# A two-layer attention and expert kernel: the first attention's first loads moved ahead of a phase seam, its router softmax split in two, and semaphore releases gathered

## What is computed

```python
x = L0_attn_x                                     # (2, 2048, 256)
xn = layernorm(x)
s = attention_full(xn, w_qkv, b_qkv, w_o) + xn    # 16 heads of 16, scale 1/sqrt(256)
g = silu(experts_bilinear(xn, router, ...))       # two branches, 8 experts of rank 64, cumulative sums
x = x + s * g
xn = layernorm(x)
s = attention_band(xn, w_qkv, b_qkv, w_out)       # keys within 64 positions, scale 1/4
g = silu(lora_experts(xn, gate_w, lora_U, lora_V))
return x + s * g
```

## Time and profile before

| | us |
|---|---|
| median of 3 runs | 2449.58 |
| lowest and highest of them | 2440.53, 2459.89 |
| the profiled execution, its own time | 2435.89 |
| its span in the trace | 2433.9 |
| first projection, about | 44 to 212 |
| full attention with its prologue | 213 to 1653 |
| prologue until the last of the first 32 maxima | 213 to 267 |
| combine of the experts | 1653 to 1970 |
| second projection, band attention, last combine | 1970 to 2070, to 2332, to 2434 |

### The profile page before, as it was taken

How to read it: one execution, slowest core, us unless ns; L and a number is a source line. 1 busy time by engine, 2 the same in 40 slices (tenths; PEclk the granted TensorE clock), 3 DMA queues, 4 the chain that set the end, 5 groups by cost and what they waited for, 6 DMA issues and landing times. The chain is left out here.

```text
span 2433.9 us, 43647 instructions
## 1 busy us (share of the span) xinstructions
PE 2211.6 (91%) x14912; PEld 1233.1 (51%) x14912; DVE 1838.5 (76%) x3240; ACT 1442.2 (59%) x2160; POOL 462.5 (19%) x673
## 2 busy tenths in 40 slices
PE   7896899999999999999999999987999987899998
PEld 4664333333333333333333333326888876666678
DVE  5664999999999999999999999912444466889745
ACT  3443377777777777777777777771222222366733
POOL 0000000000000000000000000003555520366745
PEclk9997699999999999999999999998999999699989
DMA  6888400500500501303105002007566559766654
GB/s 207 283 288 182 53 6 6 62 5 8 62 3 13 57 3 28 42 6 47 23 5 62 6 8 62 3 5 179 151 183 161 130 196 369 168 145 156 161 146 131
DMA packets 189131, 231.92 MB, mean 95 GB/s; under 512 B 72721, under 2 KB 122769, under 8 KB 186065
## 3 DMA queue, kind: packets, MB, share of 16 engines
q1 hardware_dynamic: 176048, 210.46, 35.4%
q10 hardware_dynamic: 7184, 14.10, 2.7%
q0 software_dynamic: 5728, 5.00, 0.9%
HBM read 138.97 MB, written 89.13 MB: 94 GB/s over the span
## 5 line engine op out<-in xcount | busy, mean ns | idle before, releaser
L1026 DVE TENSOR_REDUCE a_maxes<-a_ps_a 128x2 f32<-128x1024 f32 x1024 | 1202.1, 1221 | 112.9 <-PE a_ps_a L1147 109.1
L1091 ACT ACTIVATE a_prob<-a_ps_s 128x512 f32<-128x512 f32 (+1 forms) x1376 | 1035.6, 804 | 348.7 <-PE a_ps_s L1173 342.6
L1173 PE MATMUL a_ps_s<-a_Q,a_K 50*128 50x512 f32 x2048 | 593.7, 453 | 89.9 <-ACT a_prob L1091 89.7
L1147 PE MATMUL a_ps_a<-a_K,a_Q 48*128 48x512 f32 x2048 | 551.4, 455 | 26.2 <-DMA a_Q<-s_halves 14.1
L1185 PE MATMUL a_ps_o<-a_prob,a_V 128*17 128x512 f32 x4096 | 540.8, 600 | 0.1
L1173 PEld LDWEIGHTS a_ps_s<-a_Q,a_K 50*128 50x128 f32 x2048 | 277.7, 185 | 504.0 <-ACT a_prob L1091 454.9
L1147 PEld LDWEIGHTS a_ps_a<-a_K,a_Q 48*128 48x128 f32 x2048 | 245.2, 189 | 230.8 <-issue 107.9
L984 POOL DMA_DIRECT2D a_Q<-a_m_parts x128 | 64.3, 502 | 1285.5 <-DVE a_m_parts L1018 1278.9
L1653 ACT ACTIVATE a_prob<-a_ps_s 128x512 f32<-128x512 f32 (+1 forms) x256 | 135.6, 583 | 99.6 <-PE a_ps_s L1746 98.4
L1593 DVE CUSTOM_DVE_ANT_0 a_scratch<-a_ps_a,k_mask 128x256 f32<-128x256 f32 (+1 forms) x512 | 177.7, 411 | 21.5 <-PE a_ps_a L1710 19.4
L1185 PEld LDWEIGHTS a_ps_o<-a_prob,a_V 128*17 128x17 f32 x4096 | 68.1, 95 | 149.7 <-issue 97.5
(11 more groups left out here) (195 smaller groups left out, 2267.2 us busy)
## 6 DMA issues: line engine op xcount, KB each, us to landing
s_halves<-p_parts SPq DMA_DIRECT2D x32, 512.0 KB, 5.1
s_halves<-k_K SPq DMA_DIRECT2D x32, 512.0 KB, 7.4
a_Q<-s_halves SPq DMA_DIRECT2D x186, 64.0 KB, 10.7
a_K<-s_halves SPq DMA_DIRECT2D x42, 256.0 KB, 9.4
s_xT<-p_xT SPq DMA_DIRECT2D x32, 256.0 KB, 4.0
s_cT<-p_cT SPq DMA_DIRECT2D x32, 256.0 KB, 3.6
k_wb<-s_w SPq DMA_DIRECT2D x16, 512.0 KB, 7.7
c_wb<-s_w SPq DMA_DIRECT2D x16, 512.0 KB, 7.4
```

Source lines behind the costliest of these rows:

```text
L1026: nc.vector.tensor_reduce(maxes[:, :, slot, qt, kc], ps_a[:, o:o + 2 * CH].rearrange("p (z k) -> p z k", z=2), AX.X, ALU.max).then_inc(a_d ...
L1091: nc.scalar.activation(prob[:, ring:ring + len(t), :].rearrange("p r q -> p (r q)"), ps_s[:, bank:bank + len(t) * CH], ACT.Exp, scale=scal ...
L1147: last = nc.tensor.matmul(ps_a[:, o + side * CH:o + (side + 1) * CH], Q[rows, q0:q0 + P], K[rows, k0:k0 + CH], start=True, stop=True)
L1173: last = nc.tensor.matmul(ps_s[:, bank + x * CH:bank + (x + 1) * CH], K[rows, k0:k0 + P], Q[rows, q0:q0 + CH], start=True, stop=True)
```

## The change

1. **First keys and queries.** The tiles for keys and values are made ahead of the first projection (`attention_buffers`). The first queries go into the tile of the values (`VQ`). The first projection's `xT` now lies in the second half of the keys' tile, and its `parts` in the tiles `xT` and `cT` that the combine uses later, so that there is room. In the last chunk of the first projection SP waits until the stores of parts of chunk 7 of 8 have landed, issues the 6 DMAs of keys of slot 0, then the last parts' stores, then 6 DMAs of first queries and 6 of keys of slot 1, and then the last values' store.
2. **Attention's queues.** SP issues 24 DMAs of queries at the start, then waits for all 32 first maxima (`a_done`), since the values share their tile with the first queries, and only then loads the values, and the second group's keys and queries behind them. ACT no longer issues the first queries, and its four DMAs of ones come behind the router's exponential.
3. **Router softmax.** DVE does its first two steps, then four maxima, then the other five steps, then the other 28 maxima. PE turns the weights behind units 6 to 13.
4. **Seams.** The semaphores of the seven phases (and of the new holder `k4`) are put on a list and cleared by POOL inside the next block but for the last, without a release barrier of their own. The holders `k1`, `k3` and `k2` keep theirs.
5. **Last stores.** The waits on `o_stored` at the end of both attentions go. They stand in SP's queue of the following combine, ahead of the first load that could read such a row (`c == 1` in the first, behind chunk 0 in the second). The tiles `o_out` outlive the phase for that.

```diff
@@ class Names
     def release(self):
-        if self.sems:
+        if self.retired is not None:
+            self.retired.extend(self.sems)
+        elif self.sems:
             self.nc.clear_and_free_semaphores(self.sems)
             self.nc.all_engine_barrier()
+def clear_retired(nc, W):
+    if W["retired"]:
+        nc.clear_and_free_semaphores(W["retired"])
+        W["retired"].clear()
@@ phase_project
-        xT = n.sb("xT", [P, 2, 2, DK, CH], F32R) if first else KQ["own_xT"]
+        xT = A["own_xT"] if first else KQ["own_xT"]
-        parts = n.sb("parts", [P, 4, 2, CH], F32R) if first else KQ["parts"]
+            parts = [A["xT"][:, 0], A["xT"][:, 1], A["cT"][:, 0], A["cT"][:, 1]]
@@ its SP
                         first_halves(sp, 0)
+                    if first and not more and u == 1:
+                        for m in range(4):
+                            wait_apart(sp, parts_stored[m], DMA * 2 * NCH, passed)
+                        load_first_keys(sp, A["K"], S, 0, A["k_first"][0])
                     store_parts(sp, i, u)
+                    if first and not more and u == 1:
+                        load_first_queries(sp, A["Q_first"], S, 0, A["q_first"])
+                        load_first_keys(sp, A["K"], S, 1, A["k_first"][1])
@@ new
+def attention_buffers(n):
+    half = PAIR * T
+    K = n.sb("K", [P, 2 * half], F32R, side="right")
+    VQ = n.sb("VQ", [P, KT * G * VC], F32R, side="right")
+    return {"K": K, "V": f32(VQ[:]).rearrange("p (t n) -> p t n", t=KT), "Q_first": VQ[:, 0:PAIR * CH],
+            "own_xT": K[:, half:2 * half].rearrange("p (u a k t) -> p u a k t", u=2, a=2, k=DK),
...
@@ phase_attend_full, SP
-            for slot in range(PAIR):
-                load_first_keys(sp, K, S, slot, k_first[slot])
-            for qc in range(1, NCH):
+            for qc in range(NCH):
                 load_first_queries(sp, Q, S, qc, kq_loaded)
+            wait_apart(sp, a_done, 2 + NU, passed)
             for q in range(4):
                 load_v(sp, 0, q)
@@ its POOL
-            pool.wait_ge(o_stored, DMA * (NIT + 2))
+            clear_retired(nc, W)
@@ its DVE
-            router_weights_vector(nc, dve, W, r_top, r_total, r_inv, router_step, router_exp)
-            dve.wait_ge(router_step, 7)
-            for k in range(NU):
-                maximum(0, k, bank_of(0, k))
+            for part in range(2):
+                router_weights_vector(nc, dve, W, r_top, r_total, r_inv, router_step, router_exp, part)
+                for k in range(*((0, SOFT_AT) if part == 0 else (SOFT_AT, NU))):
+                    maximum(0, k, bank_of(0, k))
@@ its ACT
-            load_first_queries(act, Q, S, 0, q_first)
+            act.sem_inc(exp_done, 2)
+            router_weights_scalar(nc, act, W, router_step, router_exp)
             for side in range(2):
...
@@ its PE
-                if 0 < k <= len(w_turns):
-                    turn_weights(k - 1)
+                if SOFT_AT + 2 <= k < SOFT_AT + 2 + len(w_turns):
+                    turn_weights(k - SOFT_AT - 2)
@@ phase_attend_band, SP
-            for b in range(2):
-                wait_apart(sp, o_stored[b], DMA * NCH * NG // 2, passed)
```

More of the change, by code:

```diff
@@ L392, in phase_project @@
         cT = n.sb("cT", [P, 2, 2, DK, CH], F32R) if first else None
-        parts = n.sb("parts", [P, 4, 2, CH], F32R) if first else KQ["parts"]
+        if first:
+            parts = [A["xT"][:, 0], A["xT"][:, 1], A["cT"][:, 0], A["cT"][:, 1]]
+        else:
+            parts = [KQ["parts"][:, m] for m in range(4)]
         v_out = n.sb("v_out", [P, 2, NG2, TT, G * VC]) if first else KQ["v_out"]
@@ L476, in store_parts @@
                 sp.dma_start(S["halves"][m // 2, u, :, (m % 2) * P:(m % 2 + 1) * P, tok]
-                             .rearrange("a p t -> p a t"), f32(parts[:, m])).then_inc(parts_stored[m], DMA)
+                             .rearrange("a p t -> p a t"), f32(parts[m])).then_inc(parts_stored[m], DMA)
         def store_values(sp, i, u):
@@ L828, in load_first_queries @@
                           halves_rows(S, 0, q_part, side, slice(0, PAIR), qc * CH, CH)).then_inc(done, DMA)
+def attention_buffers(n):
[4 more added lines that the diff above has]
+            "own_xT": K[:, half:2 * half].rearrange("p (u a k t) -> p u a k t", u=2, a=2, k=DK),
+            "k_first": [n.sem(f"k_first{slot}") for slot in range(PAIR)], "q_first": n.sem("q_first")}
 FIRST_LOADS = 2 * len(HALVES_ROWS)
@@ L914, in phase_attend_full @@
         kq_loaded = n.sem("kq_loaded")
-        k_first = [n.sem(f"k_first{slot}") for slot in range(PAIR)]
-        q_first = n.sem("q_first")
         router_step = n.sem("router_step")
@@ L1146, in maximum_scores @@
                     k0 = half + slot * T + kc * CH
-                    last = nc.tensor.matmul(ps_a[:, o + side * CH:o + (side + 1) * CH], Q[rows, q0:q0 + P],
+                    last = nc.tensor.matmul(ps_a[:, o + side * CH:o + (side + 1) * CH], queries[rows, q0:q0 + P],
                                             K[rows, k0:k0 + CH], start=True, stop=True)
@@ L1293, in band_buffers @@
     KQ = {"K": n.sb("K", [P, BAND_BUFS * BAND_LONG], F32R), "Q": n.sb("Q", [P, BAND_BUFS * BAND_LONG], F32R),
+          "o_out": n.sb("o_out", [P, 2, TT, G, C]), "o_stored": [n.sem(f"o_stored{b}") for b in range(2)],
           "early": n.sem("early"), "loaded": [n.sem(f"loaded{b}") for b in range(BAND_BUFS)],
@@ L1487, in phase_attend_band @@
         o_clear = n.sem("o_clear")
-        o_stored = [n.sem(f"o_stored{b}") for b in range(2)]
+        o_stored = KQ["o_stored"]
         block = ctx.enter_context(nc.Block())
@@ L1807, in router_weights_scalar, with router_weights_vector @@
                          ).then_inc(exp_done, 1)
[L1810 removed]
+def router_weights_vector(nc, dve, W, top, total, inv, step, exp_done, part):
     groups = B * KT * 2
@@ L1814, in router_weights_vector @@
     each = lambda x: x.unsqueeze(2).broadcast_to([P, groups, E])
-    nc.vector.tensor_reduce(top, logits, AX.X, ALU.max).then_inc(step, 1)
-    dve.wait_ge(step, 1)
-    nc.vector.tensor_tensor(logits, logits, each(top), ALU.subtract).then_inc(step, 1)
+    if part == 0:
+        nc.vector.tensor_reduce(top, logits, AX.X, ALU.max).then_inc(step, 1)
+        dve.wait_ge(step, 1)
+        nc.vector.tensor_tensor(logits, logits, each(top), ALU.subtract).then_inc(step, 1)
+        return
     dve.wait_ge(exp_done, 1)
@@ L1952, in _ @@
                     wait_apart(sp, m_ready, TT * c, passed)
+                    if c == 1:
+                        wait_apart(sp, X["o_stored"], DMA * (NIT + 2), passed)
                     load_attention(c)
@@ L2248, in _ @@
                     load_turned_rows(c + BUFS)
+                    if c == 0:
+                        for b in range(2):
+                            wait_apart(sp, KQ["o_stored"][b], DMA * NCH * NG // 2, passed)
                     load_attention(c + BUFS)
@@ L2436, in recurrent_blocks @@
             "ident": n.sb("ident", [P, P]), "mask": n.sb("mask", [P, WIN]),
-            "ones": n.sb("ones", [P, P]), "half": n.sb("half", [P, TT]),
+            "ones": n.sb("ones", [P, P]), "half": n.sb("half", [P, TT]), "retired": [],
         }
```

79 lines of the change are left out of this document (42 added, 37 removed).

## The result

The changed kernel takes 2490.18 us (median of 4 runs, 2483.84 to 2494.97) against 2448.28 for the kernel before in the same comparison: a ratio of 1.0189, with a 95% interval of 1.0161 to 1.0217. It is slower by 1.9%, some 42 us, where I had forecast 2442.9. Its profiled execution has a span of 2492.1 us.

The account below looks back on a forecast made before the run. PE, busy 91%, was taken as the bound, so only seams could gain; DVE sets the attention prologue's pace. The terms summed to -6.7 us, against 2449.6 giving 2442.9, range 2427 to 2457.

Parts of the forecast that it names:

- The values' store: Projection to attention: last values' store lands at about 218.1 (216.7 to 219.7), not 211.4, behind loads issued ahead of it.
- rival A: Projection to attention: early loads run at the stores' 374 GB/s, values' store lands at 211.4; total -13.4 us, 2436.2; chance 0.20.
- the weights' seam: Seam of the weights, ahead of the first projection: one release barrier less, -0.5 us (-0.4 to -0.8).
- the term of the loads: Projection's tail: 1.97 MB of first keys and queries at 125 GB/s take 15.8 us ahead of the values' store.
- Moved softmax: Attention's prologue: five softmax steps between DVE's maxima count in full, 2.5 us; all maxima taken at 263.7 against 266.9.
- The first maxima's DMAs: Ahead of the first scores: four small POOL DMAs meet full DMA engines, +1.5 us (nothing to 4.6).
- Attention to combine: Full attention's end: the wait for the last output's store and a release barrier go, -1.0 us (-0.4 to -2.4).
- Combine to second projection: Seam between combine and second projection: one release barrier less, -0.6 us (0 to -0.8).
- Second projection to band: Seam into the band attention: one release barrier less, but the start hangs on loads, -0.3 us (0 to -0.6).
- Band to last combine: Band attention's end: block closes some 0.3 us behind SP's last store's issue, -2.4 us (-0.8 to -2.6).
- The end: Kernel's end: three release barriers become two while the clears stay, -0.2 us (0 to -0.6).
- Rival C: Projection to attention: PE's clock stays 1.00 through the shorter gap, -5.4 us more, 2437.5; chance 0.08.

Follow-up runs that it names:

- e1: Changed kernel with ten unused semaphore increments on ACT ahead of the attention's loop, so it starts on 331, not 321: 2426.5 us, ratio 0.9924 to the kernel before.
- e16: Kernel before, with POOL clearing an unused semaphore ahead of its jump to the attention block's end: drain 0.04 us, last store to SP's first load 3.59 us.
- e4: Kernel before with 256 unused semaphore increments on ACT ahead of the attention's loop, which then starts on 587: 2438.2 us, single run.

## Why the prediction was wrong

**The attention's steady part.** "The change touches nothing inside the long stages, so I read the timeline and the stretches around each seam": this is the step that failed. ACT's list lost ten instructions ahead of its loop, and I asked of those only what they cost or hide. No row of mine and none of my five cases covered the place of a loop in the list. It cost some 64 us (2490.2 less e1's 2426.5), more than every term of my sum together. In the profiled executions it is 73 us: 14 turns by 1.7 us make 24, half the clock in these turns (133 us by 0.35) some 45, and the rest, some 5, lies behind the last turn, where the clock is 0.50 for 17 us in place of 3. Without it the change does what it is for: e1 is 18.7 us faster than the kernel before in the same comparison, where my sum said 6.7; the differences at the seams add up to some 16.

**The values' store, +6.7 us later.** It landed at 211.3, not 218.1. That is the number of rival A, but not its mechanism, by which the loads fit into idle engines and the store lands 3.0 us behind its issue: it took 5.6. Windows of the changed kernel, columns as in the earlier trace rows:

```profile
193.00:195.00 2.00, 2.00 (x9) 1.56 (x10) 0.75 (x1) 0.86 (x2) 0.00 (x0) 1.00 0.98 131
...
200.00:203.00 3.00, 3.00 (x15) 2.49 (x14) 0.00 (x0) 1.47 (x3) 0.00 (x0) 1.00 1.10 381
203.00:208.40 5.40, 3.83 (x24) 2.05 (x24) 0.76 (x2) 2.05 (x3) 0.00 (x0) 1.00 1.00 166
208.40:212.00 3.60, 0.29 (x4) 0.15 (x3) 0.29 (x2) 0.00 (x0) 0.00 (x0) 0.78 0.53 144
```

Of the 6.8 us, 2.7 are that the projection itself ran ahead: the store was issued at 205.75, not 208.43, and what stands ahead of it on the queue about as much sooner. Beyond the 0.5 of the weights' seam my sum had no term for that, and it is luck. The other 4 are the term of the loads, 15.8 us. The DMA engines are full to 208.4 and busy for 0.53 of the 3.6 us behind it, so until about 210.3. From 192.5 (my 195.2, moved up by 2.7) that is 17.8 us, and less 7.1 for the stores it leaves some 11 us for 1.97 MB, about 180 GB/s, by this estimate. So the loads are slow, as I had it and A had not: from 193 to 195, with only keys' loads on full engines, the rate is 131 GB/s. But 125 was too low for all of them together, as it came from rows in which other small loads ran beside them.

Why did the projection run ahead? The clock was 0.50 for 3.4 us near 67 us in the kernel before and not in the changed one. It was so in all eight profiled kernels that have a release barrier behind the weights, and in three of the ten without. From the projection's first matmul to the store's issue are 163.9 us in the kernel before, 162.6 to 163.5 in those three, and 161.8 to 162.2 in the other seven. Whether the barrier makes it was not tried.

**Moved softmax.** 2.5 us between the maxima: measured 3.0 (43.1 less 40.1). All maxima taken: forecast 263.7 less 0.5, came at 257.6. **The first maxima's DMAs:** +1.5, with 4.6 as the far end; measured +3.6. The row was the right one: the store of 128 KB took 8.6 us in that traffic, and the four took up to 8.4. "Nearer to small DMAs under load" was the wrong choice. The slack was mis-read, though: the last of the four landed 3.3 us behind the first one's issue before, at 273.7, and the scores started 3.2 us later, where I had 0.7 or more. Now it lands 10.0 us behind that issue, 6.7 more; less the 3.2 of slack that is 3.5 of the 3.6 measured.

**Attention to combine:** -1.0 (to -2.4), measured -5.5. I had read the drain of 3.5 us and held it fixed or tied to an end; e16 shows that it hung on what stands ahead of the jump. **The weights' seam** -0.5: the projection's first matmul at 43.99 in place of 44.54, which two executions can't show, as the kernels with that barrier range from 43.1 to 44.9. **Combine to second projection** -0.6: -0.6. **Second projection to band** -0.3: 99.7 to 98.1 and 98.8 us (changed, e1), where the window holds more than the barrier, and e4, with the barrier, has 99.0: not shown. **Band to last combine** -2.4: -2.4. **The end** -0.2: -0.3.

**Rival C**, the clock held over the seam, fell: the clock went to 0.50 at 210.4, in a gap of 4.9 us, and stayed there until 278.7, though PE was back at work at 213.6. The clock struck elsewhere, in the attention's steady part, where I had taken 1.00 for granted.

## What to carry to other kernels

Before trusting that a stage is untouched, count each engine's list and find the loops: one that is longer than 256 instructions, as the one of 266 here, can stall on every branch back at some few starts, and any instruction added or removed ahead of it moves it there or away. Read the first instructions behind a loop's branch in the queue's own rows, as busy times leave them out, and keep loops under 256 instructions, or compare two versions only when their loops lie alike. And read what stood in an engine's queue ahead of an operation before its wait is called its duration.

## What the runs showed of the hardware that I had not expected

- ACT's branch back took 2.4 to 2.7 us in place of 0.24 to 0.3 in a loop of 266 instructions, for starts on 321 and 577, and not for 326, 331, 567 and 587, nor with 212 instructions on 321. The loops of DVE (146 instructions) and SP (82) took 0.3 to 0.4 in every run.
- In a stage that is otherwise dense, the clock fell from 2.4 to 1.2 GHz for 3 to 24 us behind 11 of 14 waits of PE of 1.2 to 1.5 us. The wait's length doesn't tell which (493.1 us: a wait of 1.24 and no fall; 580.0 us: 1.21 and 24 us). In the turn of 95.2 us this costs 8.2 us on top of the stall.
- POOL's drain behind a jump lasted 3.5 us in the kernel before, though POOL's last store had landed and no DMA packet moved, and 0.04 with a drain and a clear ahead of the jump (e16).
